# The x additions of pair 0 made by GpSimd instead of VectorE, in a conditioned low-rank linear kernel

## The reference

```python
y = jnp.einsum('bct,bcd->bdt', x, cond_weights[condition])
z = jnp.einsum('bsd,od->bso', y, W) + b
u = jnp.einsum('bsd,edr->ebsr', y, A)
m = jnp.einsum('ebsr,ero,e->bso', u, B, p_scores)
norm_z = jnp.linalg.norm(z, axis=-1, keepdims=True)
norm_m = jnp.linalg.norm(m, axis=-1, keepdims=True)
gamma = jnp.minimum(0.5 * norm_z / (norm_m + 1e-6), 1.0)
return x + z + gamma * m
```

## Time and profile before

| what | us |
|---|---|
| median of 3 runs | 922.59 |
| lowest and highest run | 922.33, 923.38 |
| the profiled execution, its time | 922.25 |
| the profiled execution, its span | 920.3 |
| PE busy in the span | 909.4 (99%) |
| DVE busy | 589.7 (64%) |
| ACT busy | 367.6 (40%) |
| POOL busy | 321.3 (35%) |

### The profile page before, as it was taken

How to read it: one execution, slowest core, us unless ns; L and a number is a source line. 1 busy time by engine, 2 the same in 40 slices (tenths; PEclk the granted TensorE clock), 3 DMA queues, 4 the chain that set the end, 5 groups by cost and what they waited for, 6 DMA issues and landing times.

```text
span 920.3 us, 14732 instructions
## 1 busy us (share of the span) xinstructions
PE 909.4 (99%) x4628; PEld 772.5 (84%) x4628; DVE 589.7 (64%) x930; ACT 367.6 (40%) x727; POOL 321.3 (35%) x318
## 2 busy tenths in 40 slices
PE   8999999999999999999999999999999999999997
PEld 6878888888888888888888888888888888888885
DVE  6996666556665666665576656666655757566665
ACT  6653343334334333433343343334333433433342
POOL 0024443234433244332344322443323443224432
PEclk9999999999999999999999999999999999999999
DMA  8212221122221222211222212222112222122211
GB/s 300 74 70 95 72 95 57 60 94 94 71 92 40 78 94 71 94 51 66 94 94 71 88 39 84 94 71 94 47 70 94 94 71 83 37 91 94 73 47 68
DMA packets 32744, 75.16 MB, mean 82 GB/s; under 512 B 12761, under 2 KB 13786, under 8 KB 32730
## 3 DMA queue, kind: packets, MB, share of 16 engines
q1 hardware_dynamic: 32138, 73.91, 22.8%
q10 hardware_dynamic: 448, 0.56, 0.2%
q0 software_dynamic: 144, 0.52, 0.1%
HBM read 41.42 MB, written 33.55 MB: 81 GB/s over the span
## 4 chain that ended last, share of the span: by engine, by line
PE 92%; DVE 4%; issue 1%; SPq 1%; DMA 1%; ACT 0%; POOL 0%; DVEq 0%; POOLq 0%
PE b_ps L901 35%; PE c_ps L901 18%; PE mix_ps L888 11%; PE m_ps L960 9%; PE a_ps L901 9%; PE u_ps L941 6%; PE u_ps L945 3%; DMA a_lo_raw<-in_L_ffn_A_dram 1%; DVE w_lo L640 1%; SPq L271 1%; DVE s_lo L670 0%; DVE y L649 0%; DVE w_lo_raw L616 0%; DVE w_hi_raw L630 0%; DVE w_lo_raw L623 0%
## 5 line engine op out<-in xcount | busy, mean ns | idle before, releaser
L430 ACT CAST y<-mix_ps 128x512 fp32r<-128x512 f32 x126 | 74.4, 591 | 298.5 <-PE mix_ps L888 298.5
L368 POOL TENSOR_TENSOR stats<-stats 128x1 f32<-128x1 f32 x32 | 17.8, 556 | 456.9 <-ACT squares L483 456.9
L901 PE MATMUL b_ps<-w_hi,y 128*128 128x512 f32 x512 | 168.2, 389 | 0.3 <-DVE z L746 0.3
L670 DVE TENSOR_TENSOR s_lo<-s,s_hi 128x512 fp32r<-128x512 f32 x124 | 135.7, 1114 | 4.2
L888 PEld LDWEIGHTS mix_ps<-mixer,x_in 128*128 128x128 f32 x1008 | 121.9, 191 | 7.6 <-issue 2.9
L888 PE MATMUL mix_ps<-mixer,x_in 128*128 128x128 f32 x1008 | 122.8, 275 | 1.3 <-DMA mixer<-in_L_cond_weights_dram 0.9
L443 ACT CAST s_hi<-s 128x512 fp32r<-128x512 f32 x124 | 76.6, 618 | 115.6 <-POOL s L342 93.4
L354 POOL TENSOR_TENSOR z<-z,x_in 128x512 f32<-128x512 f32 x61 | 79.2, 1299 | 113.7 <-ACT squares L464 113.7
L901 PEld LDWEIGHTS b_ps<-w_hi,y 128*128 128x128 f32 x512 | 96.1, 188 | 20.6 <-DVE z L746 0.7
L649 DVE TENSOR_TENSOR y<-mix_ps,y 128x512 fp32r<-128x512 f32 x126 | 86.4, 687 | 41.5 <-ACT s L436 39.5
L901 PE MATMUL b_ps<-w_lo,y 128*128 128x512 f32 x256 | 99.6, 389 | 0.0
(11 more groups left out here) (119 smaller groups left out, 1568.5 us busy)
## 6 DMA issues: line engine op xcount, KB each, us to landing
x_in<-in_x_dram SPq DMA_DIRECT2D x63, 512.0 KB, 3.7
out_dram<-z SPq DMA_DIRECT2D x62, 512.0 KB, 2.8
w_lo_raw<-in_L_ffn_W_dram SPq DMA_DIRECT2D x8, 256.0 KB, 6.3
mixer<-in_L_cond_weights_dram SPq DMA_DIRECT2D x126, 16.0 KB, 2.1
w_hi_raw<-in_L_ffn_W_dram SPq DMA_DIRECT2D x7, 256.0 KB, 6.2
out_dram<-z SPq DMA_DIRECT2D x3, 256.0 KB, 2.0
x_in<-in_x_dram POOLq DMA_DIRECT2D x1, 512.0 KB, 4.0
a_lo_raw<-in_L_ffn_A_dram SPq DMA_DIRECT2D x1, 512.0 KB, 8.1
```

The lines of the kernel that those rows point to most:

```text
L430: nc.scalar.copy(y_part(y_hi, r, h), source(h)).then_inc(y_hi_ready, 1)
L670: nc.vector.tensor_tensor(s_lo[:, n, :, :], s_raw(n), s_hi[:, n, :, :].bitcast(fp32), ALU.subtract).then_inc(s_lo_ready, 1)
L901: summed = nc.tensor.matmul(bank, left[:, k, :], right[:, n, k, :], start=(start and k == 0 and i == 0), stop=(stop and k == HC - 1 and i ...
```

## The change

GpSimd makes both additions of pair 0, with the helpers of the other pairs: the addition for tile 0 in two halves of 128x512, each as soon as its own half is squared, and that for tile 1 between the two norms of tile 1. The two DVE instructions are gone, and with them three waits. SP, ACT and PE have the same programs as before, and the semaphores reach the same counts.

```diff
                     opening = first and j == 0
                     if first and j == 1:
+                        residual0(0, 0, 0)
+                        residual0(0, 0, 1)
                         norm_z1(0)
+                        residual1(0, 1)
                         norm_m(0, 1)
                         norm_z0(0)
...
             make_t4(1)
             dve.wait_ge(plain_done, 8)
             nc.vector.tensor_tensor(z1[:, up_], m_ps[:, lo], bias[:, 1, :], ALU.add).then_inc(z22_ready, 1)
-            dve.wait_ge(z11_squared, 1)
-            dve.wait_ge(z12_squared, 1)
-            nc.vector.tensor_tensor(z0[:, 0, :], z0[:, 0, :], x_in[:, 0, :], ALU.add).then_inc(residual0_ready, 2)
             split_t(T4, 0)
...
             bias_p1(1, 1)
-            dve.wait_ge(z1_squared, 1)
-            nc.vector.tensor_tensor(z1[:, :], z1[:, :], x_in[:, 1, :], ALU.add).then_inc(residual1_ready, 1)
             make_gamma(0, 1)
             add_m1(0)
```

## The result

The changed kernel takes 924.6 us, the median of 14 runs (924.01 to 925.91); the kernel before took 922.82 beside it. The ratio is 1.0021, with a 95% interval of 1.0014 to 1.0028: 1.3 to 2.6 us slower, 1.9 in the middle. The prediction had 923.7 in a range of 922.3 to 924.9, slower by 1.1. The sign is right, and the size is too small by some 40%.

A forecast was written before the change was run, and what follows sets the result against it. DVE and PE were taken to run neck and neck up to 66 us, PE alone behind. Terms 1.10 - 1.13 + 0.00 + 1.16 = +1.13 us on 922.59 gave 923.7 us, range 922.3 to 924.9.

The forecast's parts named there:

- The bound: From 22.5 to 66 us DVE and PE run neck and neck and PE waits, 1.36 us idle; behind 66 only PE counts.
- Step 1: First half of tile 0: POOL's addition starts at 27.47, ahead of DVE's first T1 instruction, which starts working 1.10 us late.
- Step 2: Second half of tile 0: POOL done at 38.25, DVE's last T4 instruction at 38.12; delay 0, on the edge, bounds 0 and 1.10.
- Step 3: DVE's addition at 38.75 is gone: -1.13 us, and PE no longer waits 0.3 us for its bias instruction.
- step 4: Tile 1: POOL's addition waits for the T2 split, norm_m follows, make_gamma starts at 48.54 instead of 47.41: a +1.16 us term.
- the sum: Four terms, 1.10 - 1.13 + 0.00 + 1.16 = +1.13 us, carried by PE to the end; forecast chance 0.58.
- `norm_z1` kept its turn: Answers a rival: norm_z1, 0.11 us ahead of the T2 split, loses its turn too; +1.6 us, 924.2, chance 0.16.
- The turn at 27.7: Rival: POOL gets no turn at the first T1 instruction, or it does nothing; +0.0 to +0.1 us, 922.7, chance 0.10.
- Two turns lost: Rival: the second half of tile 0 also costs DVE 1.10 us near 38; +2.2 us, 924.8, chance 0.10.
- The gain: Rival: POOL and DVE don't hold each other in these tiles; PE gains about 0.5 us, 922.1, chance 0.06.
- The chance for slower, 0.14: Chance given to a measurably slower whole kernel, beside same 0.84 and faster 0.02.
- the prediction's own line of 1.85 us: About 0.2% of the whole kernel's time, what a measurement can tell from no change.

The follow-up runs named there:

- after_late: The changed kernel with seven more 128x512 matmuls on PE behind the first mixes; ratio 1.0034, +3.1 us.
- z0_norm_early: The changed kernel with norm_z0(0) on GpSimd moved ahead of norm_z1(0); ratio 1.0021.
- three_more: The changed kernel with three 128x1 memsets of unused columns early in VectorE's program; ratio 1.0013, 1.2 us.
- first_half_out: The changed kernel with a 128x1 GpSimd memset in place of the addition of tile 0's first half; ratio 1.0012, 1.1 us.
- halves_swapped: The changed kernel with the two halves of tile 0 added in the other order on GpSimd; ratio 1.0021.
- after_again: The changed kernel run once more, unchanged, for a second profile; ratio 1.0020.
- norm_m_first: As z0_norm_early, with norm_m(0, 1) also ahead of the addition of tile 1 on GpSimd; ratio 1.0010, +0.9 us against the kernel before.
- tile0_in_gap: The kernel before with only tile 0's addition on GpSimd, placed behind the second T4 split where VectorE reads PSUM; ratio 0.9994.
- tile0_only: The changed kernel's GpSimd addition for tile 0 only, tile 1's staying on VectorE; ratio 1.0003.

## Why the prediction was right, and where its size was off

**The bound.** Right. DVE sets the pace up to 66 us, PE behind it, and PE gave back nothing behind 66. In six profiles (the changed kernel's two, `after_late`, `z0_norm_early`, `three_more` and `first_half_out`) the span less the offset is the sum of DVE's losses and gains to 0.1 us.

**Step 1, the first half.** Right: 2.31 us at 27.73, 1.10 lost. Seven profiles with that addition ahead of it show 2.31 or 2.32.

**Step 2, the second half.** Here a term was mis-sized. It stood at 0, "on the edge", with bounds of 0 and 1.10, and measured 0.40 and 0.24 us in the changed kernel's two profiles. The loss follows the distance from POOL's start to the start of the T4 instruction: 0.29 us (`halves_swapped`) lost 0.87; 0.46 (`first_half_out`) lost 0.69; 38.17 - 37.40 = 0.77 lost 0.40; 0.93 (`after_again`) lost 0.24; 1.16 to 1.24, in the five others, lost nothing. Each is 1.16 less the distance, to 0.01. (This holds where POOL's addition isn't held itself; at 27.7 it is, and the distance of 0.21 lost 1.10.)

The step assumed that the second square moves with DVE by the same 1.10. But it hangs on PE as well: in every profile it ends 2.66 to 2.67 us behind the start of ACT's copy of the mixed tile 2 (L433, L430 before), and that copy waits for PE's mix. In the changed kernel the copy is at 34.66, 1.55 later than before, by the long first mix, while DVE is only 1.15 late at the T4 instruction: 1.55 - 1.15 = 0.40. In `after_again` it is 1.63 - 1.39 = 0.24. In `norm_m_first`, which had the long mix too, it is 1.41 - 1.40, and nothing was lost. So it is not the long mix as such that costs, but a PE that is later than DVE.

**Step 3 and step 4.** Right in mechanism and price; all of it stands 0.4 us later than forecast, by step 2. From the start of L749 to that of L690 it is 2.90 us against 1.73 from L746 to L687: +1.16, the very number of the sum. `norm_m_first` shows what the order on POOL has to do with it. PE no longer waits for `p1_biased`.

**What the sum lacked.** From the start of the first instruction of `make_gamma` to that of `add_m1(0)` it put 0.71 "as before"; it was 50.13 - 48.99 = 1.14. 0.44 us (before rounding) of the profile's loss come from that, and `three_more` takes them away with three instructions that do nothing.

**The sum by its measured terms**: 1.10 + 0.40 + 1.16 + 0.44 - 1.13 = 1.97, for the profile's 1.95 (2.0 less the offset of 0.05). Without the two missed terms it is 1.13, and `three_more`, which has neither, ended at 1.1. The runs' 1.9 agrees with this sum, but how often an execution loses the 0.40 isn't known. Both profiles of the kernel before had the short mix, so what it pays itself for a long one is not in the comparison.

**The rivals.** `norm_z1` kept its turn in every profile with this order (0.56 us, 0.11 to 0.12 ahead of the T2 split), so 0.11 is enough where 0.04 was not. The turn at 27.7 was taken wherever it was offered. "Two turns lost" is the rival that came nearest, with 0.4 in place of 1.1. The gain fell with the turns; `tile0_in_gap`, which loses only 0.19 us to a turn, has a middle of 0.6 and no gain that is shown. The chance for slower, 0.14, was too low: by the prediction's own line of 1.85 us the 1.9 is beyond it. The chances took the forecast for firm to a tenth, where its own step 2 had an open end of 1.10 just above.

## What to carry to other kernels

Moving an elementwise instruction from a full VectorE to an idle GpSimd moves no load while VectorE reads two SBUF tiles: here a GpSimd addition of 128x512 took 1.10 us of VectorE's time, where VectorE's own addition of 128x1024 took 1.13, and `tile0_only` gained nothing. Put it where VectorE reads PSUM, and ahead of nothing that somebody waits for in GpSimd's queue. Where a forecast says "just in time", read how the two sides move when something upstream is late by a microsecond, and price that.

## What the runs showed of the hardware that was not expected

- VectorE's third instruction of `make_gamma` started 0.71 us behind the second in seven profiles and 0.27 in the seven others; three 128x1 memsets far ahead of it made the difference. Nothing it waits for was late. What does it was not tried.
- The first mix took PE 3.75 us in six profiles, 2.94 in one and 2.02 in seven, with the same PE instructions up to there. Where the profile has a record of it, the slow stretch is at the lower clock level (0.50 granted from 8.40 to 11.70 in `tile0_in_gap`). The changed kernel paid 0.24 and 0.40 us for it at the last T4 instruction, `norm_m_first` nothing; no profile of the kernel before has it.
- An instruction that waits for its turn shows no idle time ahead of it: the wait is inside its own duration (2.31 in place of 1.22, 3.06 in place of 2.41). It is seen by comparing durations of one line, not in the waits.
